# Window attention and spiking layer: k goes through projection, copy, spill and stack ahead of q

## What is computed

```python
        part = x.reshape(n, H // w0, w0, W // w1, w1, c)
        part = part.transpose(0, 1, 3, 2, 4, 5).reshape(n * NW, WS, c)
        qkv = (part @ qkv_w.T + qkv_b).reshape(n * NW, WS, 3, N_HEAD, HEAD_DIM)
        q, k, v = (qkv[:, :, 0] * SCALE, qkv[:, :, 1], qkv[:, :, 2])
        attn = jnp.einsum('wihd,wjhd->whij', q, k)
        bias = bias_table[REL_IDX].transpose(2, 0, 1)
        attn = attn.reshape(n, NW, N_HEAD, WS, WS) + bias[None, None] + MASK[None, :, None]
        attn = jax.nn.softmax(attn, axis=-1).reshape(n * NW, N_HEAD, WS, WS)
        out = jnp.einsum('whij,wjhd->wihd', attn, v).reshape(n * NW, WS, c)
...
    def _L1_conv_ref(x, W, b):
...
            def step(v, x_t):
                v = v + (x_t - (v - V_RESET)) / TAU
                s = atan_spike(v - V_THRESHOLD)
                s_d = jax.lax.stop_gradient(s)
                v = V_RESET * s_d + v * (1.0 - s_d)
                return (v, s)
...
        h = jnp.einsum('tbld,hd->tblh', x, W) + b
        return lif_multistep(h)
...
    x = x + _L0_conv_ref(_gn(x), L0_conv_qkv_w, L0_conv_qkv_b, L0_conv_bias_table)
    x = x + _L1_conv_ref(_gn(x), L1_conv_W, L1_conv_b)
    return x
```

## Time and profile before

| | |
|---|---|
| median of the runs shown | 521.34 us (514.8 to 522.15, 3 runs) |
| the profiled execution, on the device | 513.7 us |
| its span in the profile | 512.0 us |
| mean granted clock of TensorE | 0.96 |
| busy time of TensorE's matmuls, VectorE, ScalarE, GpSimd | 427.2, 408.6, 376.0, 277.2 us |
| moved by the DMA engines | 61.56 MB, mean 120 GB/s |

### The profile page before, as it was taken

The page is one execution under the profiler, slowest core; times in us unless marked ns, Lnnn a source line. Parts: engine busy times, 40 slices in busy tenths (PEclk is TensorE's granted clock), DMA queues, the critical chain, the costliest instruction groups (busy, mean ns, idle before and its releaser), DMA issues.

```text
span 512.0 us, 19282 instructions
## 1 busy us (share of the span) xinstructions
PE 427.2 (83%) x7848; PEld 395.4 (77%) x7848; DVE 408.6 (80%) x872; ACT 376.0 (73%) x895; POOL 277.2 (54%) x382
## 2 busy tenths in 40 slices
PE   0274769888899899988989898989899888699996
PEld 0274768888898888988979787879798877588885
DVE  8856557798789888977978888879767787588887
ACT  2365559888898888888969787979788876746560
POOL 6353448557566766675667557656756558420000
PEclk9987669999999999999989999999999998989999
DMA  6145133545646555555464555544544551023333
GB/s 218 70 100 148 52 74 98 133 115 155 158 118 150 126 135 130 144 141 135 101 151 126 134 139 136 148 116 95 122 107 112 112 110 40 22 103 125 143 130 138
DMA packets 136780, 61.56 MB, mean 120 GB/s; under 512 B 107506, under 2 KB 125172, under 8 KB 136692
## 3 DMA queue, kind: packets, MB, share of 16 engines
q1 hardware_dynamic: 136352, 60.33, 45.6%
q10 hardware_dynamic: 340, 0.01, 0.0%
HBM read 35.13 MB, written 25.17 MB: 118 GB/s over the span
## 4 chain that ended last, share of the span: by engine, by line
PE 31%; SPq 18%; ACT 14%; DMA 11%; DVE 11%; issue 8%; POOL 6%; ACTq 0%; DVEq 0%; POOLq 0%
SPq L312 13%; DMA k_stack<-k_spill1lo 4%; DMA k_stack<-k_spill0lo 3%; SPq L307 3%; PE score_ps L916 3%; PE proj_ps L927 3%; ACT k_flat L505 3%; PE pv_ps L1038 3%; PE proj_ps L916 3%; PE pv_ps L916 3%; PE score_ps L1014 3%; PE proj_ps L929 2%; PE proj_ps L928 2%; DMA k_spill0hi<-k_flat 2%; ACT v_hi L522 2%
## 5 line engine op out<-in xcount | busy, mean ns | idle before, releaser
L449 POOL TENSOR_TENSOR p_lo<-probs,p_hi 128x512 f16<-128x512 f32 x128 | 146.5, 1166 | 128.6 <-PE pv_ps L1038 69.9
L1004 PE MATMUL score_ps<-q_stack,k_stack 96*128 96x64 f16 x1024 | 86.1, 194 | 41.7 <-ACT max_rows L595 16.7
L604 ACT ACTIVATE probs<-score_ps 128x512 f32<-128x512 f32 x128 | 76.9, 601 | 45.2 <-PE score_ps L1014 44.4
L1004 PEld LDWEIGHTS score_ps<-q_stack,k_stack 96*128 96x128 f16 x1024 | 71.9, 98 | 48.7 <-ACT max_rows L595 35.1
L778 DVE TENSOR_REDUCE neg_max<-max_ps 128x16 f16<-128x1024 f32 x64 | 78.4, 1224 | 30.9 <-PE max_ps L984 29.9
L927 PE MATMUL proj_ps<-xn_hi,w_hi 128*128 128x256 f32 x256 | 78.8, 308 | 11.1 <-DVE w_lo L731 7.2
L1000 PE MATMUL score_ps<-both_parts,bias_k 128*128 128x64 f16 x1024 | 78.2, 194 | 0.0
L605 ACT ACTIVATE p_hi<-score_ps 128x512 f16<-128x512 f32 x128 | 77.3, 604 | 0.0
L772 DVE TENSOR_TENSOR v_lo<-proj_ps,v_hi 64x256 f16<-64x256 f32 x128 | 54.2, 423 | 25.7 <-ACT v_hi L522 24.0
L928 PE MATMUL proj_ps<-xn_lo,w_hi 128*128 128x256 f32 x256 | 73.9, 289 | 0.0
L929 PE MATMUL proj_ps<-xn_hi,w_lo 128*128 128x256 f32 x256 | 73.8, 288 | 0.0
(11 more groups left out here) (130 smaller groups left out, 1196.7 us busy)
## 6 DMA issues: line engine op xcount, KB each, us to landing
xc<-in_x_dram SPq DMA_DIRECT2D x32, 256.0 KB, 3.6
q_spill<-q_flat SPq DMA_DIRECT2D x32, 256.0 KB, 2.6
q_stack<-q_spill SPq DMA_DIRECT2D x32, 256.0 KB, 3.5
out_dram<-xc SPq DMA_DIRECT2D x32, 256.0 KB, 2.2
q_stack<-q_spill SPq DMA_DIRECT2D x32, 128.0 KB, 3.6
k_spill0hi<-k_flat SPq DMA_DIRECT2D x16, 128.0 KB, 2.6
k_spill0lo<-k_flat SPq DMA_DIRECT2D x16, 128.0 KB, 3.6
k_stack<-k_spill0hi SPq DMA_DIRECT2D x32, 64.0 KB, 3.2
```

Of the source, the lines that this page charges most:

```text
L449: pool.tensor_tensor(p_lo[p][:, quads, :, :].rearrange("p g w i -> p (g w i)"), probs[:, quads, :, :].rearrange("p g w i -> p (g w i)"), p ...
L604: act.activation(probs[:, quads, :, :].rearrange("p g w i -> p (g w i)"), score_ps[:, h, :], ACT.Exp)
L1004: pe.matmul(dst, k_stack[slot][0:96, 2 * mid + q, at, :], q_stack[slot][0:96, 2 * mid + q, at, :], start=False, stop=False)
```

## The change

q and k exchange their places everywhere. TensorE projects k first, into bank 6 behind v, then q, into bank 7 behind the kept attention. ScalarE copies k first, VectorE computes k's low part first. The waits that name q's or k's parts are exchanged with them. On SP the spill of k's high part still comes first; then follow, behind the wait for q's low part, the spill of k's low part, and behind the wait for the scores the spill of q. The six k_hi pieces are followed by the four k_lo pieces, and the two q pieces come last.

```diff
--- before.py
+++ after.py
@@ -317,21 +317,21 @@
 
                 sp.wait_ge(k_hi_done, r + 1)
                 spill(k_flat, HI, k_hi_spilled, k_spill[slot][0])
-                sp.wait_ge(k_lo_done, r + 1)
-                spill_q(slot)
+                sp.wait_ge(q_lo_done, r + 1)
+                spill(k_flat, LO, k_lo_spilled, k_spill[slot][1])
                 if not is_first(r, 2):
                     sp.wait_ge(score_ps_done, 4 * (r - 2) + 4)
-                spill(k_flat, LO, k_lo_spilled, k_spill[slot][1])
+                spill_q(slot)
                 sp.wait_ge(k_hi_spilled, (r + 1) * 16)
                 stack_k(slot, 0, 0, slice(0, QUADS))
                 stack_k(slot, 32, 0, slice(0, 2))
                 stack_k(slot, 64, 0, slice(2, QUADS))
+                sp.wait_ge(k_lo_spilled, (r + 1) * 16)
+                stack_k(slot, 64, 1, slice(0, 2))
+                stack_k(slot, 32, 1, slice(2, QUADS))
                 sp.wait_ge(q_spilled, (r + 1) * 16)
                 stack_q(slot, slice(0, 64), q_spill[slot].rearrange("t r g n -> (t r) (g n)"))
                 stack_q(slot, slice(64, 96), q_spill[slot][HI].rearrange("r g n -> r (g n)"))
-                sp.wait_ge(k_lo_spilled, (r + 1) * 16)
-                stack_k(slot, 64, 1, slice(0, 2))
-                stack_k(slot, 32, 1, slice(2, QUADS))
 
             sp.wait_ge(const_step, 7)
             move_q_and_k(0, 0)
@@ -502,7 +502,7 @@
 
                 for h in range(HALVES):
                     tok = slice(h * ROWTOK, (h + 1) * ROWTOK)
-                    last = act.activation(flat[:, HI, tok], proj_ps[:, first // 2, tok], ACT.Identity,
+                    last = act.activation(flat[:, HI, tok], proj_ps[:, 1 - first // 2, tok], ACT.Identity,
                                           bias=b_cols[:, first + h:first + h + 1])
                 return last
 
...
@@ -588,7 +588,7 @@
                         if not is_last_row(row, 3):
                             normalise(row + 3, sample, nxt % 2, sample + 1, row + 3, (h,))
                         if not is_last_row(row, 2):
-                            (q_high, k_high)[h](row + 3)
+                            (k_high, q_high)[h](row + 3)
                 if v_now:
                     v_high(nxt, row + 2, 0)
                 act.wait_ge(max_turned, n + 1)
@@ -750,7 +750,7 @@
 
                 for h in range(HALVES):
                     tok = slice(h * ROWTOK, (h + 1) * ROWTOK)
-                    last = dve.scalar_tensor_tensor(flat[:, LO, tok], proj_ps[:, first // 2, tok],
+                    last = dve.scalar_tensor_tensor(flat[:, LO, tok], proj_ps[:, 1 - first // 2, tok],
                                                     b_cols[:, first + h:first + h + 1], flat[:, HI, tok], ALU.add, ALU.subtract)
                 return last
 
@@ -797,12 +797,12 @@
 
             bias_variant(0)
             bias_variant(1)
+            k_low(1)
             q_low(1)
-            k_low(1)
             dve.wait_ge(const_step, 9)
             v_low(0, 1)
+            k_low(2)
             q_low(2)
-            k_low(2)
             dve.wait_ge(const_step, 11)
             v_low(1, 2)
             sample_stats(1)
...
@@ -939,17 +939,17 @@
                     last = pe.matmul(dst, xn_lo[slot][:, tok], w_hi[:, c, cols], start=False, stop=(c == HALVES - 1))
                 return last
 
-            def project_q(slot, r):
+            def project_k(slot, r):
                 pe.wait_ge(xn_lo_done, r + 1)
                 wait(pe, v_lo_done, r)
-                project_channels(banks[6], 0, xn_hi[slot], xn_lo[slot]).then_inc(q_ps_done, 1)
-
-            def project_k(slot, r, kept=0):
+                project_channels(banks[6], C, xn_hi[slot], xn_lo[slot]).then_inc(k_ps_done, 1)
+
+            def project_q(slot, r, kept=0):
                 wait(pe, attn_kept, kept)
-                project_channels(banks[7], C, xn_hi[slot], xn_lo[slot]).then_inc(k_ps_done, 1)
+                project_channels(banks[7], 0, xn_hi[slot], xn_lo[slot]).then_inc(q_ps_done, 1)
 
             def project_v(slot, r):
-                pe.wait_ge(q_lo_done, r + 1)
+                pe.wait_ge(k_lo_done, r + 1)
                 for p in range(2):
                     last = project_tokens(proj_ps[:, 0, p * C:(p + 1) * C], p, 2 * C, slot)
                 last.then_inc(v_ps_done, 1)
...
@@ -1071,8 +1071,8 @@
                 if p == 0 and not is_first(n, 1) and not is_last_row(row):
                     project_v((k // 2 + 1) % 2, row + 1)
                 elif p == 1 and not is_last_row(row, 2):
-                    project_q(k // 2 % 2, row + 2)
-                    project_k(k // 2 % 2, row + 2, n - 2)
+                    project_k(k // 2 % 2, row + 2)
+                    project_q(k // 2 % 2, row + 2, n - 2)
                 if is_first(n, 8):
                     pe.wait_ge(bias_lo_done, variant(k, 1) + 1)
                 following = (n + 1, row + 1 if p else row, (k + 1) % BODY)
@@ -1096,7 +1096,7 @@
                 elif beside:
                     beside()
                 if p == 1 and not is_last_row(row, 2):
-                    pe.wait_ge(k_lo_done, row + 3)
+                    pe.wait_ge(q_lo_done, row + 3)
                 if not is_first(n, 2):
                     turn_attention(n - 2, p)
                 if is_last_pair(n):
```

More of the change, by code:

```diff
@@ L548, in _ @@
             act.wait_ge(setup_dve, 3)
+            k_high(1)
+            xn_high(1, 2)
             q_high(1)
-            xn_high(1, 2)
-            k_high(1)
             act.wait_ge(const_step, 9)
@@ L556, in _ @@
             bias_high(0)
+            k_high(2)
             q_high(2)
-            k_high(2)
             bias_high(1)
@@ L819, in pair @@
                 elif p == 1 and not is_last_row(row, 2):
+                    k_low(row + 3)
                     q_low(row + 3)
-                    k_low(row + 3)
                 if stage == 0 and not has_sample(s, 1):
@@ L1051, in _ @@
             pe.wait_ge(setup_dve, 4)
+            project_k(0, 0)
             project_q(0, 0)
-            project_k(0, 0)
             project_v(0, 0)
+            project_k(1, 1)
+            pe.wait_ge(q_lo_done, 1)
             project_q(1, 1)
-            pe.wait_ge(k_lo_done, 1)
-            project_k(1, 1)
             project_v(1, 1)
```

## The result

| | before | changed |
|---|---|---|
| median | 518.07 us (513.94 to 522.15, 4 runs) | 537.76 us (536.08 to 541.16, 4 runs) |
| ratio | | 1.0416, 95% interval 1.0361 to 1.047 |
| the profiled execution | 513.7 us, span 512.0 | 539.27 us, span 537.5 |
| granted clock, mean | 0.96 | 0.937 |

A forecast was written before the change was run, and what follows sets the result against it. Waits bound the kernel, through SP's issues and landing stack pieces. 7.5 us for the later last landing less 2.0 for the early k_hi spill gave +5.5 on 521.34 us: 527 us, 8 in 10 runs from 515 to 536.

The forecast's parts named there:

- Bound by SP's path: No engine is full; waits decide, with SP's issues and landing stack pieces on the chain between ScalarE's copies and TensorE's scores.
- Computing engines exchanged at 0: On TensorE, ScalarE and VectorE, first and second only change names between q and k, costed at 0.
- Step 1: On SP, k_hi's spill starts after the first ScalarE copy, about 0.7 us earlier: 2 us gained, 3.2 at best.
- Step 2: At a stack's end a q piece lands last, in 3.6 us instead of 2.93: +0.58 us each time, 7.5 us in all.
- 13 crossings: The profiled chain passes a stack's end 13 times, not 32, so the time to the last landed piece counts 13 times.
- Step 3: On SP, k_lo's spill comes 0.42 us earlier and q's 0.42 later, hidden by the six k_hi issues: cost 0.
- The slower one: Rival: at the stack's end the last q piece lands in 4.15 us, not its median; 535 us, beyond 2%, chance 0.18.
- The 0.1 us a crossing: Side estimate for q pieces last, by the skill's 2.0 us plus bytes over 436 GB/s: 1.5 us in all.

## Why the prediction was right or wrong

**Bound by SP's path: right.** Two tiny loads added to SP's queue and nothing else cost 3.4%.

**Computing engines exchanged at 0: right.** 1.0003 with all of that and nothing else.

**Step 1, the early k_hi spill, -2 us: wrong, it is 0.** With k first and the old transfers k_hi's spill starts 0.98 us earlier against the second copy, but takes 2.83 us to land instead of 2.42. It lands 1.92 us after the second copy instead of 2.50, and still its pieces start at 2.70 instead of 2.75. I had capped the gain by SP's own issues, and took 2 of 3.2 us. The cap took all of it: when the landing no longer holds SP, the second low part and two spill issues do, and the mean stays where it was. In the changed kernel the spill starts 0.91 us before the second copy's end, as forecast, but takes 3.32 us to land. SP's wait for it fell from 9.9 to 7.0 us, not below 6.

**Step 2, the tail, +0.58 us a crossing: right mechanism, too small. This is the step that failed.** With step 1 the forecast had the path grow by 0.42 us (5.5 / 13). It grew by 1.36. The last landing went from 2.88 to 3.78 us, by 0.90 and not 0.67; its longest went from 4.0 to 5.2 us. The rest of the path added 0.46 us where I had subtracted 0.09 (0.14 by the 0.49 us that the first q issue really took in that row) and the gain of step 1; most of it (0.31) stands ahead of the first k_hi piece, where SP now waits 22.1 us for scores. That part isn't the tail's in every case: in the three other kernels with this tail and two stacks the path grew by 0.9 to 1.1 us, and the first k_hi piece moved by 0.12 us at most.

**The count, 13 crossings: nearly what the chain shows, but no price.** The changed kernel's chain crosses 14 ends of stacks. The two loops of two rows each that I read from one turn were not the whole of it, since the old chain has a turn of one row as well. The three other kernels with the tail cross 17, 12 and 15 ends, at ratios of 1.0257, 1.0389 and 1.0339, so the number of crossings doesn't go with the time. 13 crossings at the measured 1.36 us give 17.7 of the 25.5 us. By the line of the experiments a us of path costs 0.61 us a row, some 17 us over 28 rows instead of 13: 1.36 us give 23 of the 25, the forecast's 0.42 us only 7. So of the missing 20 us, 12 to 16 are the size of the path's growth, and 2 to 6 the price of a us of path.

**TensorE's clock: the forecast had no term for it.** Of the 44.4 us at the lower level in rows 3 to 30, TensorE's work on the chain fills 39.0; before, it fills 6.8. If this work took half the time at the upper level, (39.0 - 6.8) / 2 = 16 us of the 25 hang on the clock: an estimate and an upper bound, since another chain would have taken over some of it. It isn't to be added to the price of the path, since the drops come behind pauses of TensorE, and its waits for stacks grew with the tail from 22.2 to 34.1 us. In the three other kernels with the tail the lower level lasted 20 to 24 us, and their spans grew by 16 to 17 us instead of 25.5. No run held the clock, so how much of the 0.61 is the path itself and how much the clock behind its waits stays open.

**Step 3, the spills' order at 0: right** (0.9971).

**Rivals.** The slower one named nearly the right time (535 us) for a reason that didn't occur in that form: the last piece's landing is 3.6 us in the median and 3.78 in the mean, not 4.15. That it came so near was luck.

The 0.1 us a crossing that the prediction worked out beside its own sum is too small for this tail: with 256 KB put just in front of them, the same 128 KB landed after 3.6 us instead of 2.7, a step of 0.9 us. The Trainium skill (DMA: Bandwidth & Descriptors, section Anatomy of one DMA) gives 2.0 us and the bytes over 436 GB/s as a fit for a single transfer on GpSimd's path, where these are several on SP's; 256 KB over that rate are 0.6 us, an estimate.

## What to carry to other kernels

In a queue of transfers that is waited for as a whole, put the pieces with the most data early and the small ones last; the other order cost 2.6 to 4.2% here. Where a path through such a queue decides, a microsecond on it should be priced by an experiment with a dummy issue or two, since a count of crossings in the chain of the kernel before gave too little here. Where the change makes TensorE pause more often, look at the granted clock of the stretch before summing up. Starting the first transfer earlier gains nothing when a later wait in the same queue still holds what follows.

## What the runs showed that I had not expected

A tiny load of 256 bytes costs SP's queue about as much as one of 32 KB: two took 0.89 us, four pieces of k_lo 1.89 us. One such pair in each of 32 rows cost 3.4% of the kernel.

TensorE's granted clock fell with the waits: 0.96 over the span before, 0.937 with the change, and the same 7848 matmuls were busy 440.0 us instead of 427.2. The products with the probabilities (L1038) took 203 to 204 ns instead of 196 to 198. Which pauses bring a drop and which don't wasn't tried.
